# Attention scores on two row tiles of 64 array rows, their rows laid out in bands of 16 through device memory

## The chip, the cores and the metric

The kernel runs on one core of one Trainium2 chip. The metric is the device time of one execution in microseconds (us). TensorE (PE) multiplies matrices, VectorE (DVE) reduces and combines, ScalarE (ACT) evaluates exponentials and copies, GpSimd (POOL) does small elementwise work, and SyncE (SP) issues nearly all DMAs. Each engine works through its own instructions in order, and semaphores order the engines among each other.

## The reference

One transformer layer on x of shape (8, 256, 128). First comes attention with 16 heads of size 8, over 512 context positions and the element's own 256 positions; then a mixture of 8 experts, of which each token takes two. The change concerns the scores of the attention:

```python
q, k, v = (qkv[0], qkv[1], qkv[2])                 # (B, 16, 256, 8)
k = jnp.concatenate([extra_k, k], axis=2)          # 512 context keys + 256 own
attn = jnp.einsum('bhnd,bhmd->bhnm', q * scale, k)
attn = jax.nn.softmax(attn, axis=-1)
out = jnp.einsum('bhnm,bhmd->bhnd', attn, v)
out = out.transpose(0, 2, 1, 3).reshape(B, N, C)
x = x + out @ w_proj.T + b_proj
```

## The kernel before, in words

The attention runs over 32 **quads**: for each of the 8 batch elements (`b`), four groups (`r`, or `t`) of four heads. All engines follow the same outer loop, `steps`: in step `s` (with `b, r = divmod(s, 4)`) PE computes the exponentials' scores of quad `s` and the scores for the row maxima of quad `s+2`, so the maxima run two steps ahead.

**Rows of the matmul.** Keys and queries have 32 rows per quad (4 heads of 8). Each is split into a rounded part and a rest (`parts`), and the product of three combinations (high with high, high with rest, rest with high) gives back the precision. So the stationary and moving operands `keys` and `blocks` have 96 rows of products, and four more rows (`SUM_ROWS`) subtract the row maxima. `blocks` holds the queries masked per head (`masked`, made by `mask_queries`), so that one operand of 128 rows serves four heads at once. The rows are moved from `parts` and `masked` into `keys` and `blocks` by DMAs from SBUF to SBUF, in `spread_rows` and `spread_blocks` on SP: three DMAs of 96 KB, three of 128 KB and one of 8 KB per quad. They are issued at the end of a step, when all exponential matmuls of quad `s` are out (`exp_filled`), for quad `s+4`, whose maxima PE starts at the beginning of step `s+2`.

**A step on PE** has six groups `i`. Each holds two halves of one maximum unit (`max_half`, unit `w = i`) and two exponential units (`exp_unit`), in the order half, exp, half, exp. After group 1 stand the value products (`pv_tile`, 128 rows by 32 columns, four column tiles at a time) of the second half of quad `s-1`, after group 4 those of the first half of quad `s`. Before groups 3 and 4 stand small transposes (`transpose_maxima`, `transpose_out`).

**Who waits for whom.** ACT turns each of the 12 exponential units from a PSUM bank (`exp_ps`, two of them) into `probs`; DVE reduces each of the 6 maximum units from a pair of banks (`max_ps`, two pairs) into `max_part`. The merged maxima go from DVE to POOL (split in two), to PE (transposed), to ACT (`maxT`), and by a DMA of 8 KB on SP into `blocks`; the first exponential unit of the next step waits for it (`max_in`). POOL makes `parts` and `masked` for later batch elements (`split_context` in its steps r = 2, `split_own` in r = 3), in two buffers.

Of the kernel before, what the change touches and what calls it, by code (L numbers as in the profile page):

```python
# [85 lines left out]
OWN = NC_  # L86


def attend(nc, m, d):

# [11 lines left out]
    with ExitStack() as ctx:  # L102
# [13 lines left out]
        bias_added = sem("bias_added")  # L116
        rows_in, max_in = [sem(f"rows_in{t}") for t in range(T)], [sem(f"max_in{t}") for t in range(T)]
# [16 lines left out]
        parts = sb("parts", [P, 2, 2, NC_ + 2 * N], F32R)  # L134
        keys = sb("keys", [P, T, KEYS], F32R)
        masked = sb("masked", [P, 2, 2, G, N])
        head_hot, mask = sb("head_hot", [P, HEADS]), sb("mask", [P, G])
        blocks = sb("blocks", [P, T, G, N], F32R)
        ctx_v, own_v = sb("ctx_v_sb", [P, 2, CT, C]), sb("own_v", [P, 2, QT, C])
        value_cols = sb("value_cols", [P, T, KT, G, ROWS])  # L140
        max_part, rowmax = sb("max_part", [P, 2, 2, G, QT]), sb("rowmax", [P, 2, G, QT])
# [21 lines left out]
        def spread_blocks(engine, q):  # L163
            c, t = divmod(q, T)
            for j, part in enumerate((0, 0, 1)):
                engine.dma_start(blocks_f[ROWS * j:ROWS * (j + 1), t], masked[ROWS * t:ROWS * (t + 1), c % 2, part])\
                      .then_inc(rows_in[t], 16)

        def mask_queries(engine, c, part):
            spread = [P, G, N]  # L170
            return engine.tensor_tensor(masked[:, c % 2, part],
                                        parts_f[:, c % 2, part, KEYS:KEYS + N].unsqueeze(1).to_broadcast(spread),
                                        mask[:].unsqueeze(2).to_broadcast(spread), ALU.mult)

        rows_spread = lambda q: 16 * (6 + 7 * (q // T))

        @block.sync
        def _(sp):
# [3 lines left out]
            def spread_rows(q):  # L182
                c, t = divmod(q, T)
                high, rest = parts_f[:, c % 2, 0], parts_f[:, c % 2, 1]
                head = slice(ROWS * t, ROWS * (t + 1))
                for j, part in enumerate((high, rest, high)):
                    sp.dma_start(keys_f[ROWS * j:ROWS * (j + 1), t, :], part[head, 0:KEYS]).then_inc(rows_in[t], 16)
                if q:
                    spread_blocks(sp, q)
                if c:  # L190
                    sp.dma_start(blocks_f[SUM_ROWS:SUM_ROWS + 2, t], blocks_f[SUM_ROWS + 2:SUM_ROWS + 4, t])\
                      .then_inc(rows_in[t], 16)
# [927 lines left out]
```

## Time and profile before

| | |
|---|---|
| time, median of 3 runs | 581.93 us (579.75 to 582.76) |
| profiled execution, its own time | 579.1 us |
| its span in the trace | 577.5 us |
| PE busy | 498.9 us, 86% |
| DVE busy | 353.9 us, 61% |
| ACT busy | 292.7 us, 51% |
| POOL busy | 196.0 us, 34% |
| device memory read, written | 16.58 MB, 4.72 MB |

The attention takes the first 370 us or so of the span, the experts the rest. A busy PE is one with a matmul in its pipeline, which is not the same as one at its peak. The profiled execution lies 2.8 us under the median of the runs.

### The profile page before, as it was taken

The numbers are of one execution on the slowest core, as the hardware profiler recorded it, in microseconds if no ns is written. First come the engines' busy times: TensorE is split into PE (matmuls) and PEld (weight loads), VectorE is DVE, ScalarE is ACT, GpSimd is POOL, SyncE is SP. The second block draws the span as 40 slices with busy tenths as digits, with TensorE's granted clock in tenths as the row PEclk, the third lists the DMA queues.
The fourth block names the chain that finished last, engine by engine and source line by source line (L and its number), as shares of the span: only waits on it lengthen the run. The fifth ranks groups of instructions, "written<-read, shape, count | busy, mean of one in ns | idle before, by whom it ended". The sixth has DMA issues, their size and how long they took to land. (4 is left out here: it accounts for less than half of the span.)

```text
span 577.5 us, 10586 instructions
## 1 busy us (share of the span) xinstructions
PE 498.9 (86%) x3467; PEld 322.9 (56%) x3468; DVE 353.9 (61%) x646; ACT 292.7 (51%) x584; POOL 196.0 (34%) x381
## 2 busy tenths in 40 slices
PE   3479999999999999999999998555499999999940
PEld 1346666666666666666565663244447666666630
DVE  7597687777777787777777770368524333333316
ACT  2136667767767677676776767421023333333310
POOL 7151241331422412411400000103317776677630
PEclk9999999999999999999999999865569999999995
DMA  6802434445244344342332300160101111111116
GB/s 168 185 25 72 94 88 108 95 105 134 75 113 121 87 120 104 91 115 64 76 72 58 90 3 2 36 184 0 14 10 43 41 41 38 39 36 43 42 51 189
DMA packets 32078, 44.39 MB, mean 77 GB/s; under 512 B 5484, under 2 KB 20460, under 8 KB 32036
## 3 DMA queue, kind: packets, MB, share of 16 engines
q1 hardware_dynamic: 27076, 36.88, 25.7%
q0 software_dynamic: 2560, 5.25, 3.6%
q10 hardware_dynamic: 2400, 1.70, 1.2%
q8 instruction: 26, 0.43, 0.3%
q14 instruction: 16, 0.13, 0.1%
HBM read 16.58 MB, written 4.72 MB: 37 GB/s over the span
## 5 line engine op out<-in xcount | busy, mean ns | idle before, releaser
L426 DVE TENSOR_REDUCE max_part<-max_ps 128x2 f32<-128x1024 f32 (+1 forms) x192 | 231.3, 1221 | 79.6 <-PE max_ps L519 42.1
L385 ACT ACTIVATE probs<-exp_ps 128x512 f32<-128x512 f32 x384 | 207.4, 591 | 77.5 <-PE exp_ps L541 72.0
L541 PE MATMUL exp_ps<-blocks,keys 128*128 128x512 f32 x384 | 160.9, 421 | 4.5 <-ACT probs L385 2.3
L519 PE MATMUL max_ps<-keys,blocks 128*128 128x512 f32 x256 | 109.9, 436 | 10.1 <-DMA blocks<-masked 7.0
L541 PEld LDWEIGHTS exp_ps<-blocks,keys 128*128 128x128 f32 x384 | 71.7, 187 | 44.8 <-ACT probs L385 18.5
L551 PE MATMUL pv_ps<-probs,value_cols 128*32 128x256 f32 x1536 | 96.3, 383 | 0.0
L986 DVE TENSOR_TENSOR hidden<-up_ps,silu 128x512 f32<-128x512 f32 x40 | 27.7, 692 | 84.4 <-PE up_ps L1076 82.4
L302 POOL CAST maxes<-rowmax 128x8 fp32r<-128x8 f32 x32 | 6.3, 198 | 178.6 <-DVE rowmax L432 178.6
L519 PEld LDWEIGHTS max_ps<-keys,blocks 128*128 128x128 f32 x256 | 48.4, 191 | 30.2 <-DVE max_part L426 19.2
L551 PEld LDWEIGHTS pv_ps<-probs,value_cols 128*32 128x32 f32 x1536 | 43.3, 109 | 39.4 <-issue 17.1
L879 ACT ACTIVATE hiddenT<-at_ps 128x512 f32<-128x512 f32 x40 | 23.9, 597 | 77.2 <-PE at_ps L1093 68.7
L524 PE MATMUL max_ps<-keys,blocks 128*128 128x256 f32 x256 | 56.1, 303 | 1.6 <-DVE max_part L426 1.6
L524 PEld LDWEIGHTS max_ps<-keys,blocks 128*128 128x128 f32 x256 | 42.8, 189 | 10.2 <-DVE max_part L426 7.5
L1073 PE MATMUL gate_ps<-gate,xT 128*128 x80 | 44.4, 638 | 2.9 <-DVE xT L978 1.5
L1085 PEld LDWEIGHTS t_ps<-down,hiddenT 128*128 128x128 f32 x320 | 38.9, 192 | 14.0 <-issue 14.0
L823 POOL DMA_INDIRECT x_in<-h_rows,source_now x40 | 39.6, 989 | 17.1 <-issue 16.5
L1085 PE MATMUL t_ps<-down,hiddenT 128*128 x320 | 42.6, 276 | 2.1 <-ACT hiddenT L879 1.5
L847 POOL DMA_INDIRECT pick_outs<-y_out,target_now x40 | 39.6, 991 | 12.5 <-issue 10.2
L875 ACT ACTIVATE silu<-gate_ps 128x512 f32<-128x512 f32 x40 | 23.8, 596 | 37.5 <-PE gate_ps L1073 36.1
L1076 PE MATMUL up_ps<-up,xT 128*128 x80 | 42.6, 615 | 0.0
L264 POOL COPY value_cols<-ctx_v_sb 128x128 f32<-128x128 f32 x32 | 9.7, 304 | 68.8 <-PE pv_ps L551 66.8
L1076 PEld LDWEIGHTS up_ps<-up,xT 128*128 128x128 f32 x80 | 15.8, 197 | 20.2 <-issue 20.2
(148 smaller groups left out, 473.4 us busy)
## 6 DMA issues: line engine op xcount, KB each, us to landing
blocks<-masked SPq DMA_DIRECT2D x93, 128.0 KB
keys<-parts SPq DMA_DIRECT2D x96, 96.0 KB
ctx_v_sb<-ctx_v_dram SPq DMA_DIRECT2D x8, 256.0 KB, 2.9
gate<-gateT_dram SPq DMA_DIRECT2D x8, 256.0 KB, 2.8
up<-upT_dram SPq DMA_DIRECT2D x8, 256.0 KB, 2.6
y_in<-pick_outs SPq DMA_DIRECT2D x8, 256.0 KB, 4.9
raw<-ctx_kT_dram SPq DMA_DIRECT2D x7, 256.0 KB, 2.8
h_rows<-h SPq DMA_DIRECT2D x4, 256.0 KB, 4.9
```

Source lines behind the costliest of these rows:

```text
L385: act.activation(probs[par][:, k, 2 * half:2 * half + 2], exp_ps[u % 2][:].rearrange("p (g n) -> p g n", n=N), ACT.Exp).then_inc(exp_done, 1)
L426: vec.reduce_max(out, bank, axis=AX.X).then_inc(max_done, 1)
L519: mm = pe.matmul(max_ps[w % 2][:, half * BANK:(half + 1) * BANK], blocks[:, t, w, half * P:(half + 1) * P], keys[:, t, 0:NC_], start=True, ...
L524: mm = pe.matmul(max_ps[w % 2][:, first:first + N], blocks[:, t, 2 * (w - G) + half, i * P:(i + 1) * P], keys[:, t, NC_:KEYS], start=True, ...
L541: pe.matmul(exp_ps[u % 2][:], keys[:, t, k * P:(k + 1) * P], blocks[:, t, 2 * half:2 * half + 2, :], start=True, stop=True).then_inc(exp_f ...
L551: mm = pe.matmul(pv_ps[ROWS * g:ROWS * (g + 1), 0:N], value_cols[:, t, k, g, :], probs[q % 2][:, k, g, :], start=(k == 0), stop=(k == KT - 1))
L823: pool.indirect_dma_start(x_in[:, r, :], None, h_dram, bass.IndirectOffsetOnAxis(ap=source_now[:, r:r + 1], axis=0))\
L847: pool.indirect_dma_start(outs_dram, bass.IndirectOffsetOnAxis(ap=target_now[:, before2:before2 + 1], axis=0), y_out[:, before2, :], None) ...
L986: vec.tensor_tensor(hidden[:, r % 2, :], up_ps[r % 2][:], silu[:, r % 2, :], ALU.mult)\
L1073: pe.matmul(gate_ps[r % 2][:], xT[:, r % 2, :], m.gate[:, bass.ds(e, 1), :].rearrange("p a i -> p (a i)"), start=True, stop=True).then_inc ...
L1076: pe.matmul(up_ps[r % 2][:], xT[:, r % 2, :], m.up[:, bass.ds(e, 1), :].rearrange("p a i -> p (a i)"), start=True, stop=True).then_inc(up_ ...
L1085: mm = pe.matmul(y_ps[:, 0:C], hiddenT[:, r % 2, c, :], down[:, bass.ds(e, 1), c, :].rearrange("p a h -> p (a h)"), start=(c == 0), stop=( ...
```

## The change

The rows of a quad are laid out anew. A quad becomes two halves `a` of two heads each (`PAIR`), and each half has its own 64 rows (`TILE`): three bands of 16 rows (`BAND`) of products, 48 in all, and four more rows (two of which take the maxima). Half 0 uses rows 0 to 63, half 1 rows 64 to 127. The matmul instructions keep their number and their sizes in columns; each now contracts over 48 rows (maxima) or 64 rows (exponentials) instead of 128. On PE the order within a group becomes: maximum of half 1, exponential of half 0, maximum of half 0, exponential of half 1.

The rows come about in another way. Once per batch element SP writes `parts` and `masked` to device memory (`write_bands`: three DMAs of 384 KB and three of 256 KB, from 128 partitions each, with a destination of 8 blocks of 16 rows), waits for all six (`bands_in`), and reads the 48 rows of each half back (`read_bands`: four DMAs per quad, two of 96 KB and two of 144 KB). `parts` and `masked` now have one buffer, the device memory has two. The maxima go into `blocks` in two DMAs of 4 KB instead of one of 8 KB. `masked` has half as many columns, and at the start all of `masked` comes from 128x512 instead of 128x1024 operations; the DMAs that ACT issued at the start (`spread_blocks(act, 0)`) go.

```diff
+PAIR = G // 2
+TILE = P // 2
+BAND = PAIR * D
+MAX_ROW = 3 * BAND
...
+        key_bands = nc.dram_tensor("key_bands", (2, 2 * T, 3, BAND, KEYS), F32, kind="Internal").ap()
+        query_bands = nc.dram_tensor("query_bands", (2, 2 * T, 3, BAND, PAIR * N), F32, kind="Internal").ap()
...
+            def write_bands(c):
+                if c >= 2:
+                    for t in range(T):
+                        sp.wait_ge(rows_in[t], rows_spread(T * (c - 2)))
+                for j, part in enumerate((0, 1, 0)):
+                    sp.dma_start(key_bands[c % 2, :, j], parts_f[:, part, 0:KEYS]).then_inc(bands_in[c % 2], 16)
+                for j, part in enumerate((0, 0, 1)):
+                    sp.dma_start(query_bands[c % 2, :, j], masked[:, part]).then_inc(bands_in[c % 2], 16)
+
+            def read_bands(q):
                 c, t = divmod(q, T)
...
+                sp.wait_ge(bands_in[c % 2], bands_written(c))
+                for a in range(2):
+                    rows = slice(TILE * a, TILE * a + MAX_ROW)
+                    sp.dma_start(blocks_f[rows, t], query_bands[c % 2, 2 * t + a].rearrange("j i n -> (j i) n"))\
+                      .then_inc(rows_in[t], 16)
+                    sp.dma_start(keys_f[rows, t], key_bands[c % 2, 2 * t + a].rearrange("j i n -> (j i) n"))\
                       .then_inc(rows_in[t], 16)
...
-                    sp.dma_start(blocks_f[SUM_ROWS:SUM_ROWS + 2, q], maxT_f[:, (s + 1) % 2, :]).then_inc(max_in[q], 16)
+                    for a in range(2):
+                        row = TILE * a + MAX_ROW
+                        sp.dma_start(blocks_f[row:row + 2, q], maxT_f[2 * PAIR * a:2 * PAIR * (a + 1), (s + 1) % 2, :])\
+                          .then_inc(max_in[q], 16)
+                if r == 0 and b + 1 < B and b >= 0:
+                    sp.wait_ge(ctx_split, 2 * (b + 1) + 2)
+                    sp.wait_ge(own_split, 4 * (b + 1))
+                    write_bands(b + 1)
...
-                    c = (s + T) // T
-                    sp.wait_ge(ctx_split, 2 * c + 2)
-                    sp.wait_ge(own_split, 4 * c)
                     sp.wait_ge(exp_filled, (s + 1) * XUNITS)
-                    spread_rows(s + T)
+                    read_bands(s + T)
...
             def split_context(c):
                 pool.wait_ge(keysT_in[c % 2], 16 * (c // 2 + 1))
-                if c >= 2:
-                    for t in range(T):
-                        pool.wait_ge(rows_in[t], rows_spread(T * (c - 2)))
+                if c:
+                    pool.wait_ge(bands_in[(c - 1) % 2], bands_written(c - 1))
                 split(ctx_split, 2 * c, c, slice(0, NC_))
...
-                    mm = pe.matmul(max_ps[w % 2][:, half * BANK:(half + 1) * BANK], blocks[:, t, w, half * P:(half + 1) * P],
-                                   keys[:, t, 0:NC_], start=True, stop=True)
+                    g, i = divmod(w, QT)
+                    mm = pe.matmul(max_ps[w % 2][:, a * BANK:(a + 1) * BANK], blocks[rows, t, g, i * P:(i + 1) * P],
+                                   keys[rows, t, 0:NC_], start=True, stop=True)
...
-                pe.matmul(exp_ps[u % 2][:], keys[:, t, k * P:(k + 1) * P], blocks[:, t, 2 * half:2 * half + 2, :],
-                          start=True, stop=True).then_inc(exp_filled, 1)
+                pe.matmul(exp_ps[a][:], keys[rows, t, k * P:(k + 1) * P], blocks[rows, t], start=True, stop=True)\
+                  .then_inc(exp_filled, 1)
...
-                    for half in range(2):
+                    for a in range(2):
                         if has_scores(s + 2):
-                            max_half(s + 2, i, half)
+                            max_half(s + 2, i, 1 - a)
                         if has_scores(s):
-                            exp_unit(s, 2 * i + half)
+                            exp_unit(s, 2 * i + a)
```

The instructions of SP in the first step of a batch element and at the beginning of the next, before:

```order
L161 DMA raw<-ctx_kT_dram 128x512
L221 DMA blocks<-maxT 2x4x256
L224 DMA gate<-gateT_dram 128x512
L187 DMA keys<-parts 32x768 x3
L166 DMA blocks<-masked 32x1024 x3
L191 DMA blocks<-blocks 2x1024
L180 DMA ctx_v_sb<-ctx_v_dram 128x4x128
L221 DMA blocks<-maxT 2x4x256
```

The same place of SP in the changed kernel:

```order
L169 DMA raw<-ctx_kT_dram 128x512
L233 DMA blocks<-maxT 2x2x256 x2
L190 DMA key_bands<-parts 8x16x768 x3
L192 DMA query_bands<-masked 8x16x512 x3
L241 DMA gate<-gateT_dram 128x512
L199 DMA blocks<-query_bands 48x512
L201 DMA keys<-key_bands 48x768
L199 DMA blocks<-query_bands 48x512
L201 DMA keys<-key_bands 48x768
L183 DMA ctx_v_sb<-ctx_v_dram 128x4x128
L233 DMA blocks<-maxT 2x2x256 x2
```

The six writes stand between the step's maxima and the reads of the next element's first quad, and the next step's maxima (the last row) stand behind both.

SP at the start, before (the first rows of quads 0 and 1):

```order
L180 DMA ctx_v_sb<-ctx_v_dram 128x4x128
L187 DMA keys<-parts 32x768 x6
L166 DMA blocks<-masked 32x1024 x3
L187 DMA keys<-parts 32x768 x3
L166 DMA blocks<-masked 32x1024 x3
```

SP at the start in the changed kernel:

```order
L183 DMA ctx_v_sb<-ctx_v_dram 128x4x128
L190 DMA key_bands<-parts 8x16x768 x3
L192 DMA query_bands<-masked 8x16x512 x3
L199 DMA blocks<-query_bands 48x512
L201 DMA keys<-key_bands 48x768
L199 DMA blocks<-query_bands 48x512
L201 DMA keys<-key_bands 48x768
```

Where three direct copies of quad 0's keys went out first, the whole batch element is now written before the first row is read back.

## Rows read from the trace of the kernel before

**Rows 1.** The page: busy time of the engines; PE in 40 slices.

```profile
PE 498.9 (86%) x3467; PEld 322.9 (56%) x3468; DVE 353.9 (61%) x646; ACT 292.7 (51%) x584; POOL 196.0 (34%) x381
...
PE   3479999999999999999999998555499999999940
```

**Rows 2.** Timeline of PE in one step (start, duration, count).

```profile
240.71 0.40 PE L541 MATMUL exp_ps<-blocks,keys 128*128 128x512 f32 x1
241.04 1.50 PE L551 MATMUL pv_ps<-probs,value_cols 128*32 128x256 f32 x24
242.47 0.50 PE L524 MATMUL max_ps<-keys,blocks 128*128 128x256 f32 x2
242.81 0.39 PE L541 MATMUL exp_ps<-blocks,keys 128*128 128x512 f32 x1
```

**Rows 3.** Timeline of ACT, same step.

```profile
237.65 0.38 ACT L374 ACTIVATE pv_sb<-pv_ps 128x256 f32<-128x256 f32 x1 [0.86 <-PE pv_ps L551]
...
239.51 2.25 ACT L385 ACTIVATE probs<-exp_ps 128x512 f32<-128x512 f32 x4
243.24 1.09 ACT L385 ACTIVATE probs<-exp_ps 128x512 f32<-128x512 f32 x2 [1.49 <-PE exp_ps L541]
```

**Rows 4.** Timeline of DVE, same step.

```profile
241.20 1.22 DVE L426 TENSOR_REDUCE max_part<-max_ps 128x4 f32<-128x1024 f32 x1
243.48 1.23 DVE L426 TENSOR_REDUCE max_part<-max_ps 128x4 f32<-128x1024 f32 x1 [1.07 <-PE max_ps L524]
```

**Rows 5.** Timeline: first exponential matmul of steps 0 and 30; value products of last steps.

```profile
37.40 0.40 PE L541 MATMUL exp_ps<-blocks,keys 128*128 128x512 f32 x1
...
346.39 0.89 PE L541 MATMUL exp_ps<-blocks,keys 128*128 128x512 f32 x2 [0.30 <-ACT probs L385]
...
348.54 1.50 PE L551 MATMUL pv_ps<-probs,value_cols 128*32 128x256 f32 x24
...
358.13 1.50 PE L551 MATMUL pv_ps<-probs,value_cols 128*32 128x256 f32 x24
```

**Rows 6.** Timeline of weight loads, after a block of value products.

```profile
242.47 0.30 PEld L524 LDWEIGHTS max_ps<-keys,blocks 128*128 128x128 f32 x2 [0.41 <-DVE max_part L426]
```

**Rows 7.** Timeline: start of a batch element's first step on PE; DMA issues on SP.

```profile
243.51 0.40 PE L519 MATMUL max_ps<-keys,blocks 128*128 128x512 f32 x1
...
249.84 0.65 SPq L221 DMA_DIRECT2D blocks<-maxT  x1
253.98 1.81 SPq L187 DMA_DIRECT2D keys<-parts  x3
...
270.73 0.65 SPq L221 DMA_DIRECT2D blocks<-maxT  x1
```

**Rows 8.** Windows: engines, granted clock, busy share of 16 DMA engines, GB/s.

```profile
4.00:5.00 1.00, 0.00 (x0) 0.00 (x0) 0.32 (x2) 0.00 (x0) 1.00 (x2) 1.00 1.11 371
265.50:266.00 0.50, 0.50 (x5) 0.43 (x3) 0.50 (x1) 0.50 (x2) 0.41 (x2) 1.00 0.83 197
272.00:272.25 0.25, 0.25 (x5) 0.11 (x8) 0.21 (x3) 0.25 (x1) 0.00 (x0) 1.00 0.10 33
...
385.00:400.00 15.00, 4.16 (x18) 3.99 (x18) 12.02 (x33) 1.51 (x2) 0.87 (x2) 0.50 0.00 0
575.50:576.50 1.00, 0.00 (x0) 0.00 (x0) 0.00 (x0) 0.00 (x0) 0.00 (x0) 0.50 0.90 255
```

**Rows 9.** DMA issues: KB each, median us from issue to landing.

```profile
out_dram<-x ACTq DMA_DIRECT2D x4, 256.0 KB, 2.5
```

**Rows 10.** Timeline of the start, all engines.

```profile
13.25 2.44 DVE L171 TENSOR_TENSOR masked<-parts,mask 128x1024 f32<-128x1024 f32 x2
...
13.43 4.06 SPq L187 DMA_DIRECT2D keys<-parts  x6
...
21.55 1.19 PE L519 MATMUL max_ps<-keys,blocks 128*128 128x512 f32 x2 [7.03 <-DMA blocks<-masked]
...
26.61 0.72 PE L519 MATMUL max_ps<-keys,blocks 128*128 128x512 f32 x2 [0.82 <-DVE max_part L426]
```

More of the change, by code:

```diff
@@ L116, in attend @@
         bias_added = sem("bias_added")
+        bands_in = [sem(f"bands_in{i}") for i in range(2)]
         rows_in, max_in = [sem(f"rows_in{t}") for t in range(T)], [sem(f"max_in{t}") for t in range(T)]
@@ L255, in split_own @@
                     pool.wait_ge(own_split, 4 * c - 3 + part)
[L256 removed]
+                    mask_queries(pool, part).then_inc(own_split, 1)
             def fill_values(q):
@@ L277, in _ @@
                                pattern=[[-1, P]], channel_multiplier=1).then_inc(ident_done, 1)
-            for t in range(T):
-                pool.memset(blocks[:, t].bitcast(F32), 0.0).then_inc(blocks_zero, 1)
+            pool.memset(blocks[:].bitcast(F32), 0.0).then_inc(blocks_zero, 1)
             split_context(0)
@@ L510, in project_values, with max_half @@
                 mm.then_inc(v_filled, 1)
-            def max_half(q, w, half):
-                t = q % T
-                if w == 0 and half == 0:
+            def max_half(q, w, a):
+                t, rows = q % T, slice(TILE * a, TILE * a + MAX_ROW)
+                if w == 0 and a:
                     pe.wait_ge(rows_in[t], rows_spread(q))
-                if half == 0:
+                if a:
                     wait_for(pe, max_done, q * MUNITS + w - 1)
                 if w < G:
-                    mm = pe.matmul(max_ps[w % 2][:, half * BANK:(half + 1) * BANK], blocks[:, t, w, half * P:(half + 1) * P],
-                                   keys[:, t, 0:NC_], start=True, stop=True)
+                    g, i = divmod(w, QT)
+                    mm = pe.matmul(max_ps[w % 2][:, a * BANK:(a + 1) * BANK], blocks[rows, t, g, i * P:(i + 1) * P],
+                                   keys[rows, t, 0:NC_], start=True, stop=True)
                 else:
                     for i in range(QT):
-                        first = half * BANK + i * N
-                        mm = pe.matmul(max_ps[w % 2][:, first:first + N],
-                                       blocks[:, t, 2 * (w - G) + half, i * P:(i + 1) * P], keys[:, t, NC_:KEYS],
-                                       start=True, stop=True)
-                if half:
+                        first = a * BANK + i * N
+                        mm = pe.matmul(max_ps[w % 2][:, first:first + N], blocks[rows, t, w - G, i * P:(i + 1) * P],
+                                       keys[rows, t, NC_:KEYS], start=True, stop=True)
+                if a == 0:
                     mm.then_inc(max_filled, 1)
```

93 lines of the change are left out of this document (39 added, 54 removed).

## The prediction

> **What bounds the kernel now.** I read the page first: PE is busy 86% of the span and sits at 9 tenths in every slice of the attention [rows 1]. That invites the reading that PE sets the pace, so the second view is PE's timeline. From the first exponential matmul of step 0 at 37.40 to that of step 30 at 346.39 there are 308.99 us, 10.30 us a step. Steps 30 and 31 hold no maxima at all, half of PE's score work is gone, and yet the same place in two successive steps (the first value products) is 358.13 - 348.54 = 9.59 us apart [rows 5]. So PE's score matmuls are worth at most 10.30 - 9.59 = 0.71 us a step. What does set the pace is seen in ACT's timeline: four exponentials in 2.25 us, 0.56 us each, 6.7 us for twelve; and around each of the two blocks of value products ACT stands idle, 0.86 us before `pv_sb` and 1.49 us before the next exponential [rows 3]. The block takes 1.43 us of PE from its start at 241.04 to the next group at 242.47, and there are only two banks of scores in flight, so ACT runs out; the next exponential matmul starts another 0.34 us later, at 242.81 [rows 2]. DVE waits in the same place, 1.07 us [rows 4]. The pace is the loop of ACT, two banks and the value products, with DVE close by.
>
> **The matmuls.** Their number and columns stay; what can go is the time in which an exponential waits for the half before it. In the rows that is the 0.34 us after each block [rows 2], for ACT and for DVE, twice a step: at most 0.68 us, which is also what the steps without maxima say (0.71). Against it: `transpose_maxima` and `transpose_out` use the whole array and now stand between matmuls of half height. What a change of the array's division costs is seen after the value products (128x32): the next weight load comes 0.41 us after PE's previous one [rows 6], although the reduction it is put down to, of two units before, was long over. Four such changes a step are new, up to 1.6 us of PE; ACT's `maxT` and `pv_sb` copies cover most of it. I take a gain of 0.4 us a step (0.68 less a share of the four changes), 30 x 0.4 = 12 us in all, between 21 us (0.71) and nothing.
>
> The page "TensorEngine Tiling (Array Packing)" of the Trainium skill (Overview) gives up to 2x for a contraction of at most 64 rows. A pair of 512 columns each takes 0.43 us at 2.4 GHz, so by that alone the 12 pairs of a step would give back 2.6 us, and the sum would lose 77 us. The trace does not let it through, by the 9.59 us above. Its Key Properties say that changing the tiling mode drains TensorE; by that rule, the 0.41 us are a drain, and the trace agrees.
>
> **The writes, a new wait on SP.** Three DMAs of 384 KB and three of 256 KB are 1.97 MB. Nothing in the trace writes such rows to device memory, so the time T is bounded. Copies of the same 3 KB rows between SBUF tiles moved 197 GB/s at 0.83 of 16 engines' time, 14.8 GB/s an engine; loads 371 GB/s at 1.11, 20.9 GB/s an engine; the final stores lie between, 255 at 0.90, 17.7 [rows 8]. How many engines work at once? The DMA of `maxT`, two rows at its destination, moved its 8 KB in one quarter of a microsecond at a share of 0.10, 1.6 engines' worth [rows 8]: I read this as an engine for each of the two leading rows. A destination of 8 blocks then has 8 engines. T is 1.97 MB over 8 engines: 16.6 us at 14.8, 11.8 us at 20.9, 13.9 us at 17.7. I take 14. On all 16 engines T would be 8.3 to 5.3 us.
>
> The page "DMA: Bandwidth & Descriptors" of the Trainium skill (section on why a DMA increments its semaphore by 16) says that the engine count is the largest number up to 16 that divides both slowest dimensions; for 128 and 8 that is 8. No row shows a DMA with a leading 8.
>
> **Where SP stands meanwhile.** I count from the start of a batch element's first step on PE, 243.51, to the issue of the maxima, 249.84: 6.3 us [rows 7]. Two issues of 0.65 follow, to 7.6. From issue to data pass 1.4 us (issued at 270.73, moved from 272.00 to 272.25) [rows 7, 8], so data flow from 9.0 to 9.0 + 14 = 23.0; the landing of a store adds some 0.3 (2.5 us for 256 KB, of which 1.4 are the start and 0.9 the data) [rows 9], 23.3. Only then does SP pass `bands_in` and issue four reads at 0.60 to 0.62 each (three in 1.81 us) [rows 7], to 25.8, and one load, to 26.2. Behind them in SP's order stand the maxima of the *next* step. Their second DMA is issued at 26.85 and lands 1.5 later, at 28.35. PE wants them at the beginning of the second step after, at 2 x 9.9 = 19.8, plus 0.2 for the first maximum: 20.0. The first maxima of the new element want the read rows there too, and these arrive at 25.2 + 1.4 + 0.4 = 27.0. So PE, ACT and DVE stand 28.35 - 20.0 = 8.35 us, or T - 5.65. It happens once for each element that is still to be written, 7 times: 58 us. Nothing gives it back, since every step behind it has ACT's full length. Before, the rows went directly from SBUF to SBUF, and SP waited for no data between two sets of them.
>
> A stop of 8 us may also lower TensorE's clock. At the beginning, after a long idle, two 512-column matmuls took 1.19 us, later 0.72 [rows 10]; the thin stretch after the attention has the granted clock at 0.50, the 1.2 GHz level [rows 8]. If a stop does this, one block of value products (1.43 us) takes twice its time: 1.2 us each (between 0 and 2.4), 8 us.
>
> **The start.** The masked queries end at 13.25 + 2.44 = 15.69 [rows 10]; at half the columns at about 14.5. Data flow from 15.9 to 29.9, landed 30.2; the fourth read is issued at 32.1 and in at 33.9. The first maxima matmul was at 21.55 and waited for its rows then too [rows 10]: 12.3 us later, or T - 1.65. What follows it to step 0 is the same chain of reductions.
>
> POOL's new wait for `bands_in` in `split_context` falls into the same stop, a step or more before its product is used; nothing. The smaller `masked` operations are on POOL, 34% busy; nothing, their cover is its idle time.
>
> **The sum.** 579.1 (profiled execution, span 577.5 and 1.6 around it) - 12 + 58 + 8 + 12 = 645; the median of the runs shown lies 2.8 above the profiled one: 648. With T from 11.8 to 16.6, a step's gain from 21 to 0 and the clock from 0 to 17: 579.1 - 21 + 43 + 0 + 10 = 611, and 579.1 + 77 + 17 + 15 = 688.
>
> **The rivals.**
> - *All 16 engines write, and the gain stands* (not slower). T of 5.3 us: no stop, a start of +4: 579.1 - 12 + 4 = 571; at 8.3 us 7 x 2.65 + 7 - 12 gives 592. It turns where 7 (T - 5.65) + (T - 1.65) = 12, at T = 6.7 us, 296 GB/s. For it: loads did move 371 GB/s. Against it: only with 16 engines at full use, and the `maxT` row. 12 in 100 for faster or the same, 8 in 100 for 575 to 600.
> - *PE is the bound after all*: 12 pairs of 512 columns, 0.43 us each at the 2.4 GHz of the granted clock (1.00 in the windows of the attention [rows 8]), would take half: 2.6 us a step less, 77 us, which would turn 648 into 571. Against it stand steps 30 and 31. 2 in 100.
> - *The two halves do not overlap, or the changes of mode are all paid*: up to 1.6 us a step, 48 us, on top of the stops: 648 + 12 + 48 = 708, or some 640 where the writes are fast. For it the 0.41 us; against it ACT's copies. 10 in 100.
> - *A shorter stop*, because the six DMAs share engines better or SP is through sooner: 600 to 625. 13 in 100.
> - The forecast, 625 to 675: 55 in 100.
>
> **How the numbers follow.** About 0.5%, 3 us, is what a measurement of this kernel tells from none. Faster: 0.12, same: 0.03, slower: 0.85. The range from 592 to 690 leaves out most of the 16-engine rival below and the worst mode changes above.
>
> **What would show it.** Right: once per element, SP idle over 10 us for the DMAs of the bands, and right behind it one stop of PE of 6 to 11 us; the DMA share near 0.5 during the writes; the first maxima matmul near 34; between the stops steps of 9.6 to 10.2 us. A DMA share near 1 in the writes, or SP passing within 8 us, would make it wrong; so would steps under 9 us, or over 11.

## The result, and the profile after

The changed kernel takes 657.75 us (median of 4 runs, 651.18 to 660.53) where the kernel before, on the same chip, takes 582.35 (median of 4, 579.75 to 583.17). The ratio is 1.1287, with a 95% interval from 1.1187 to 1.1388: slower. The profiled execution took 660.21 us, with a span of 658.3; its mean granted clock is 0.868.

The page of the changed kernel, beside [rows 1]: busy time, the slices of PE, of its granted clock and of the DMA engines.

```profile
PE 519.4 (79%) x3467; PEld 299.9 (46%) x3468; DVE 353.7 (54%) x646; ACT 294.6 (45%) x584; POOL 180.4 (27%) x378
...
PE   2069899599699699699599699985565999999960
...
PEclk9999789788788989889979878976555999999995
DMA  5452413513622622532511421006001111111117
```

PE's slices are no longer even: from the eighth on, every third is a 5 or a 6. Its clock slices, too, are broken into 7s and 8s. DVE and ACT have the same busy time as before; what came in is standing still.

SP's timeline around one batch element's writes, issues alone:

```profile
259.71 1.27 SPq L233 DMA_DIRECT2D blocks<-maxT  x2
261.56 2.97 SPq L190 DMA_DIRECT2D key_bands<-parts  x3
264.57 5.43 SPq L192 DMA_DIRECT2D query_bands<-masked  x3
270.04 0.98 SPq L241 DMA_DIRECT2D up<-upT_dram  x1
275.44 0.33 SPq L199 DMA_DIRECT2D blocks<-query_bands  x1
275.81 0.42 SPq L201 DMA_DIRECT2D keys<-key_bands  x1
276.28 0.42 SPq L199 DMA_DIRECT2D blocks<-query_bands  x1
276.74 0.42 SPq L201 DMA_DIRECT2D keys<-key_bands  x1
...
277.68 1.38 SPq L233 DMA_DIRECT2D blocks<-maxT  x2
```

From the first write's issue to the first read's are 13.9 us. Only the last 4.4 of them (271.02 to 275.44) are idle waiting of SP for `bands_in`; the six writes and the load behind them took SP 9.4 us to issue. The maxima of the next step stand behind the reads and go out 18.0 us after their predecessors.

PE's timeline after that, and two other places: the start (beside [rows 10] and [rows 5]), and a block of value products in a step without a stop (beside [rows 2]).

```profile
34.75 0.79 PE L531 MATMUL max_ps<-keys,blocks 48*128 48x512 f32 x2 [18.70 <-DMA keys<-key_bands]
...
50.68 1.19 PE L553 MATMUL exp_ps<-blocks,keys 64*128 64x512 f32 x2
...
57.98 2.79 PE L563 MATMUL pv_ps<-probs,value_cols 128*32 128x256 f32 x24
...
280.06 0.79 PE L531 MATMUL max_ps<-keys,blocks 48*128 48x512 f32 x1 [6.45 <-DMA keys<-key_bands]
...
300.64 1.50 PE L563 MATMUL pv_ps<-probs,value_cols 128*32 128x256 f32 x24
302.07 0.39 PE L536 MATMUL max_ps<-keys,blocks 48*128 48x256 f32 x1
302.08 0.50 PE L553 MATMUL exp_ps<-blocks,keys 64*128 64x512 f32 x1
```

PE stands 6.45 us for `keys<-key_bands`. The block of value products at 57.98 took 2.79 us where it takes 1.50 at full clock: the attention begins at the lower level. At 302.07 and 302.08 a matmul for maxima and one for exponentials, on the two row tiles, start 0.01 us apart: the overlap is real, and the exponential no longer stands 0.34 us behind the maximum. The first exponential matmul is at 50.68, where it was at 37.40.

The windows of the changed kernel: the writes, the stop, and the two stretches behind it.

```profile
265.00:271.00 6.00, 6.00 (x51) 3.54 (x50) 5.27 (x7) 4.82 (x11) 1.56 (x5) 1.00 0.51 185
...
278.00:280.00 2.00, 0.00 (x0) 0.00 (x0) 0.00 (x0) 0.00 (x0) 0.00 (x0) 0.50 0.90 199
280.00:286.80 6.80, 6.74 (x36) 3.29 (x36) 2.45 (x2) 2.72 (x6) 0.00 (x0) 0.54 0.43 112
286.80:295.00 8.20, 7.89 (x66) 4.33 (x58) 5.59 (x8) 5.73 (x13) 2.50 (x5) 1.00 0.20 55
```

While the writes flow, the DMA engines are busy 0.51 of 16, that is 8 engines. In the stop, the clock falls to 0.50 (1.2 GHz), and for most of the 6.8 us of work behind it it stays there.

The chain of waits between 100 and 400 us of the changed kernel (in total, times, longest):

```profile
ACT probs L395 <- PE exp_ps L553: 99.1, 79, 7.6
DVE max_part L436 <- PE max_ps L531: 84.4, 43, 7.7
...
PE max_ps L531 <- DMA keys<-key_bands: 38.2, 6, 6.9
```

Six stops in this stretch, one for each element, and PE's releaser is the rows read back.

**Where the 80.8 us of span went.** Three places divide it: the first exponential matmul, the first statistics of the second layer norm (DVE, at 370.57 before and 448.66 after), and the end. The start is 13.3 us longer. The attention between the two places takes 397.98 us in place of 333.17: 64.8 more. The rest takes 2.7 more. In the attention DVE's idle times at the seven stops are 3.57, 7.71, 6.67, 6.80, 7.01, 7.17 and 6.46, 45.4 us. The distance between the first value products of successive steps, over an element's four steps at full clock, was 10.32, 10.74, 10.49 and 10.04; with row tiles it is 9.95, 10.38, 10.22 and 9.60: 0.36 us a step less, 10 us over 28 steps. (These four come from the version with both edits below; in the changed kernel itself the second always has a stop, and its other steps at full clock are 9.95, 10.21 to 10.24 and 9.58.) What is left, 64.8 - 45.4 + 10 = 29.4 us, I put to the clock; the experiments test that.

### The profile page after: what moved, and what is told of

It reads as the page before. It is cut to its first block and busy times, and to the rows that moved or that the text cites. A ratio compares the mean times of both kernels' runs of the same rounds, so it can differ in the third digit from the quotient of the medians.

```text
span 658.3 us, 10585 instructions
## 1 busy us (share of the span) xinstructions
PE 519.4 (79%) x3467; PEld 299.9 (46%) x3468; DVE 353.7 (54%) x646; ACT 294.6 (45%) x584; POOL 180.4 (27%) x378
## 5 line engine op out<-in xcount | busy, mean ns | idle before, releaser
L553 PE MATMUL exp_ps<-blocks,keys 64*128 64x512 f32 x384 | 171.3, 515 | 11.4 <-ACT probs L395 10.3
L531 PE MATMUL max_ps<-keys,blocks 48*128 48x512 f32 x256 | 114.3, 505 | 62.3 <-DMA keys<-key_bands 59.6
L563 PE MATMUL pv_ps<-probs,value_cols 128*32 128x256 f32 x1536 | 113.3, 435 | 0.0
L553 PEld LDWEIGHTS exp_ps<-blocks,keys 64*128 64x128 f32 x384 | 70.9, 201 | 47.1 <-issue 20.1
L531 PEld LDWEIGHTS max_ps<-keys,blocks 48*128 48x128 f32 x256 | 49.2, 218 | 93.4 <-DMA keys<-key_bands 42.4
L563 PEld LDWEIGHTS pv_ps<-probs,value_cols 128*32 128x32 f32 x1536 | 47.5, 121 | 48.9 <-issue 28.4
L536 PE MATMUL max_ps<-keys,blocks 48*128 48x256 f32 x256 | 48.5, 319 | 1.0 <-DVE max_part L436 1.0
L835 POOL DMA_INDIRECT x_in<-h_rows,source_now x40 | 39.4, 986 | 17.2 <-issue 16.6
L536 PEld LDWEIGHTS max_ps<-keys,blocks 48*128 48x128 f32 x256 | 32.2, 196 | 17.1 <-issue 9.3
L384 ACT ACTIVATE pv_sb<-pv_ps 128x256 f32<-128x256 f32 x32 | 12.3, 384 | 36.4 <-PE pv_ps L563 36.4
```

The source lines that it names most:

```text
L531: mm = pe.matmul(max_ps[w % 2][:, a * BANK:(a + 1) * BANK], blocks[rows, t, g, i * P:(i + 1) * P], keys[rows, t, 0:NC_], start=True, stop= ...
L536: mm = pe.matmul(max_ps[w % 2][:, first:first + N], blocks[rows, t, w - G, i * P:(i + 1) * P], keys[rows, t, NC_:KEYS], start=True, stop=True)
L553: pe.matmul(exp_ps[a][:], keys[rows, t, k * P:(k + 1) * P], blocks[rows, t], start=True, stop=True)\
L563: mm = pe.matmul(pv_ps[ROWS * g:ROWS * (g + 1), 0:N], value_cols[:, t, k, g, :], probs[q % 2][:, k, g, :], start=(k == 0), stop=(k == KT - 1))
L835: pool.indirect_dma_start(x_in[:, r, :], None, h_dram, bass.IndirectOffsetOnAxis(ap=source_now[:, r:r + 1], axis=0))\
```

## The experiments

The theory going in was the prediction's: the stop and the late start are the time of the writes on 8 engines, seen through SP's order; the row tiles themselves gain a little. Rivals: the loss is in the row tiles (changes of the array's division, no overlap) or in the clock.

**Sixteen engines for the writes.** The buffers in device memory get 128 leading rows, so that the writes' destinations do too; within a half the rows then lie head channel by head channel, which changes no sum:

```diff
-        key_bands = nc.dram_tensor("key_bands", (2, 2 * T, 3, BAND, KEYS), F32, kind="Internal").ap()
+        key_bands = nc.dram_tensor("key_bands", (2, P, 3, KEYS), F32, kind="Internal").ap()
...
-                    sp.dma_start(key_bands[c % 2, :, j], parts_f[:, part, 0:KEYS]).then_inc(bands_in[c % 2], 16)
+                    sp.dma_start(key_bands[c % 2, :, j, :], parts_f[:, part, 0:KEYS]).then_inc(bands_in[c % 2], 16)
```

> The writes get a destination whose leading dimension is 128 instead of 8; bytes, issues and their place stay. Theory (a DMA uses as many engines as its leading dimension allows, and SP's wait behind the writes makes the stop): the DMA share in the writes goes from 0.50 to near 1, SP's time from the first write's issue to the first read from 13.9 us to 8 to 9, the stop of DVE from 6.4 to 7.7 us to 0.5 to 2, the start 5 to 6 us earlier, and the time to 595 to 615 us. Rival (the rate into device memory or out of SBUF bounds the writes, not the number of engines): share near 1 but 13.9 us stays within 2 us, time above 640.

Measured: 596.49 us (594.69 to 598.47), ratio 1.0257 (1.0214 to 1.03). A window in its writes, and SP's issues:

```profile
220.00:224.00 4.00, 3.67 (x28) 2.29 (x32) 2.76 (x4) 2.84 (x6) 0.41 (x2) 1.00 1.02 394
```

```profile
218.90 1.35 SPq L190 DMA_DIRECT2D key_bands<-parts  x3
220.29 2.63 SPq L192 DMA_DIRECT2D query_bands<-masked  x3
...
227.03 0.32 SPq L199 DMA_DIRECT2D blocks<-query_bands  x1
```

The same bytes at the same place in SP's order now move at 394 GB/s (all traffic of the window) with a share of 1.02, and the first read is issued 8.1 us after the first write in place of 13.9. Up to the last steps, which have no maxima, no stop of DVE is longer than 2.7 us, and the first maxima matmul is at 27.4 in place of 34.75. So 61 of the 75 us hang on how many engines the writes get.

The page "DMA: Bandwidth & Descriptors" of the Trainium skill (section on why a DMA increments its semaphore by 16) has the engines as the largest number up to 16 that divides both slowest dimensions, 8 for 128 and 8, 16 for 128 and 128. The trace agrees, with 0.51 and 1.02.

**The writes earlier in SP's order.** Only their place changes, from behind the step's maxima to the beginning of the element's first step:

```diff
             def step(s, b, r):
+                if r == 0 and b + 1 < B and b >= 0:
+                    sp.wait_ge(ctx_split, 2 * (b + 1) + 2)
+                    sp.wait_ge(own_split, 4 * (b + 1))
+                    write_bands(b + 1)
```

> The six writes are issued at the beginning of the element's first step instead of behind the maxima of it, 7 us earlier; still 8 engines. Theory (SP's place makes the stop): the writes take the same 13.9 us, the stop falls below 1 us, the start stays as it is, time 590 to 615. Rival (the stop comes of the amount of data in the queues, wherever the writes stand): the stop stays at 5 us or more and the time within 15 us of the changed kernel's. If the clock falls only because of the stops, the granted clock rises from 0.87 to about 0.93.

Measured: 648.30 us (642.77 to 652.11), ratio 1.1178 (1.1107 to 1.1248). The theory of SP's order missed: the stop did not go, it moved, and the rival's figures came. The mean clock, 0.877 to 0.898 over the executions, did not rise to 0.93 either. SP's issues, ACT's copy of the maxima and PE's timeline, then PE's chain of waits between 100 and 360 us:

```profile
241.81 3.16 SPq L190 DMA_DIRECT2D key_bands<-parts  x3
245.02 5.33 SPq L192 DMA_DIRECT2D query_bands<-masked  x3
...
251.46 1.59 SPq L237 DMA_DIRECT2D blocks<-maxT  x2
```

```profile
245.69 0.36 ACT L389 ACTIVATE maxT<-shared_ps 8x256 fp32r<-8x256 f32 x1
```

```profile
256.08 0.80 PE L553 MATMUL exp_ps<-blocks,keys 64*128 64x512 f32 x2 [5.85 <-DMA blocks<-maxT]
```

```profile
PE exp_ps L553 <- DMA blocks<-maxT: 34.6, 6, 6.1
```

SP no longer waits for the end of the writes ahead of the maxima, but the issues themselves hold it. The maxima are ready at 246.05, when ACT's copy ends, and go out at 251.46, 5.4 us later; in steps without writes this takes 0.03 us. The six issues took 8.5 us, and the load behind them 1.0 where it takes 0.4 elsewhere. The 8 KB then land 4.6 us after the first of their two issues. In the version without a trip through memory (below), an exponential that waited for the same pair started 2.5 us after the first issue (326.35 to 328.84), so the transfer itself is some 2 us slower behind the writes. So six writes on 8 engines delay what stands behind them in two ways, and the larger is the time for which their issues hold the engine.

The page "DMA: Bandwidth & Descriptors" of the Trainium skill (section on queues, rings and completion order) says that each DMA engine consumes the descriptors of a ring in their order. The 2 us fit that, but no run here separates it from the mere sharing of the DMA engines.

**Both edits together.**

> Both edits. Theory: no stop, as with the early writes alone, so only the start gives more, 5 to 6 us: 584 to 609 us. Rival (fast writes still leave a part of a stop that the early ones don't): below the early one by more than 10 us.

Measured: 591.48 us (589.54 to 595.49), ratio 1.0198 (1.0144 to 1.0251). The expectation took for granted that the early writes alone leave no stop, and they did leave one; the 57 us between the two runs are its price and that of the start. No stop is left here, and the full steps are the 9.95, 10.38, 10.22 and 9.60 given above. Here the row tiles are seen without a stop: the start costs 43.28 - 37.40 = 5.9 us, and the attention takes 336.3 us where it took 333.2. The gain of 10 us a run is thus not just missing but overdrawn by 3; the 13 us against it go with a clock of 0.96 (windows below).

**The writes from POOL.** Built on the last: the writes of elements 1 to 7 are issued by GpSimd, behind its own `split_own`:

```diff
+                pool.wait_ge(ctx_split, 2 * c + 2)
+                pool.wait_ge(own_split, 4 * c)
+                write_bands(c)
```

> The kernel with writes on 16 engines, but those of elements 1 to 7 issued by GpSimd, right after it has made the rows, so they stand in neither SP's order nor its DMA queue. Theory (what the early writes left was the maxima's DMA standing behind the writes in one queue): no stop over 1 us, time 584 to 595, like that with both edits. Rival (the DMA engines themselves are shared, whatever the queue): maxima still late by 2 us or more, time above 600.

Measured: 594.70 us (591.75 to 594.96), ratio 1.0248 (1.0191 to 1.0305). No stop, the first maxima matmul at 27.29. The maxima are now issued within 0.03 us of ACT's copy in every step, where with both edits they are up to 2.4 us late behind the writes. Yet in four of the seven elements their packets begin to move only 1.9 to 2.4 us after the issue, where 1.25 is usual; with both edits it is 1.6 to 2.2. With 16 engines nothing more was to be had from another queue. Writes on 8 engines in another queue were not run.

**No trip through memory.** The bands go from SBUF to SBUF as before the change, but 16 rows at a time, 12 DMAs a quad, with `parts` and `masked` double:

```diff
+                    for j, (kp, qp) in enumerate(((0, 0), (1, 0), (0, 1))):
+                        rows = slice(TILE * a + BAND * j, TILE * a + BAND * (j + 1))
+                        sp.dma_start(keys_f[rows, t, :], parts_f[head, c % 2, kp, 0:KEYS]).then_inc(rows_in[t], 16)
+                        sp.dma_start(blocks_f[rows, t], masked[head, c % 2, qp]).then_inc(rows_in[t], 16)
```

> The two row tiles as in the change, but the bands go directly from SBUF to SBUF, twelve DMAs of 16 rows per quad, with two buffers for parts and masked as before; no device memory. Theory (row tiles give 0.7 us a step at full clock; the way over memory cost the start and the stops): first maxima matmul at 22 to 25 us, steps of 9.6 to 9.9, no stop, 21 us gained less some 10 for the clock: 565 to 580 us. Rival (twelve issues a step fill SP, 7.2 us of 9.6, and the last rows come late): PE waits for rows every step, time above 590.

Measured: 609.93 us (609.02 to 620.29), ratio 1.0508 (1.0432 to 1.0584). Two rows of its SP, and two of its chain of waits between 100 and 350 us:

```profile
261.60 0.59 SPq L192 DMA_DIRECT2D blocks<-masked  x1
262.23 0.59 SPq L191 DMA_DIRECT2D keys<-parts  x1
```

```profile
PEld exp_ps L542 <- DMA blocks<-maxT: 13.2, 12, 1.7
...
PE exp_ps L542 <- DMA blocks<-maxT: 6.9, 7, 1.4
```

The expected 565 to 580 us missed by 30, and the rival's figure (above 590) came. There is no 8 us stop, but twelve issues of 0.59 us back to back take 7.5 us of each step's 10, the maxima stand behind them, and steps last 9.95 to 13.7 us. The start shows it best: the first maxima matmul is early, at 24.79, and the first exponential is late, at 48.62. Writing whole bands to memory and reading 48 rows at 0.42 us an issue was the cheaper way for SP.

**No overlap of the halves.** Both halves of the score matmuls take the rows of tile 0, so that the products of tile 1's heads are left out:

```diff
-                t, rows = q % T, slice(TILE * a, TILE * a + MAX_ROW)
+                t, rows = q % T, slice(0, MAX_ROW)
...
-                rows = slice(TILE * a, TILE * (a + 1))
+                rows = slice(0, TILE)
```

> Both halves of a quad are computed from the rows of half 0, so that no two score matmuls lie on different rows of the array; the output is that of other scores, the work of every engine and every wait are the same. Theory (the overlap is worth about 0.7 us a step at full clock): steps of 10.2 to 10.6 us outside the stops instead of 9.6, time 675 to 690. Rival (the step is ACT's and DVE's alone, overlap is worth nothing): within 5 us of the changed kernel.

Measured: 739.6 us, from 713.08 to 763.57; its executions lie too far apart for a ratio, and only the kind of loss is read. Even 713.08 us is above the expected 675 to 690. The profiled execution is the one of 763.57 us, with a mean clock of 0.756; the one of 713.08 has 0.837, the changed kernel 0.868 to 0.888. A window of its attention, and its PE:

```profile
100.00:200.00 100.00, 99.84 (x515) 57.30 (x514) 50.30 (x62) 49.31 (x96) 16.41 (x38) 0.64 0.29 81
```

```profile
151.29 0.79 PE L531 MATMUL max_ps<-keys,blocks 48*128 48x512 f32 x1
151.88 0.62 PE L553 MATMUL exp_ps<-blocks,keys 64*128 64x512 f32 x1
152.31 0.62 PE L531 MATMUL max_ps<-keys,blocks 48*128 48x512 f32 x1
152.74 0.62 PE L553 MATMUL exp_ps<-blocks,keys 64*128 64x512 f32 x1
```

PE is busy 99.84 of 100 us, yet its clock is at 0.64 in the mean: 72 of these 100 us at the lower level, where 512 columns take 0.43 us. The size of 0.64 belongs to this execution; that the clock is lower than in the changed kernel holds for all four. I had expected the overlap's loss and the changes of mode alone. That the clock falls while PE is busy almost without a gap was in no theory.

The page "TensorE: Matmul & The Clock Gate" of the Trainium skill (Part 1) sets the clock by how busy TensorE has been. This measurement differs if busy means time in matmuls: 99.84% of the window held only 0.64.

**Half height alone.** The kernel before, with its score matmuls on rows 0 to 63 (the products of the other rows are left out), nothing else changed; so no overlap, no bands, the four changes of the array's division:

```diff
-                pe.matmul(exp_ps[u % 2][:], keys[:, t, k * P:(k + 1) * P], blocks[:, t, 2 * half:2 * half + 2, :],
+                pe.matmul(exp_ps[u % 2][:], keys[0:64, t, k * P:(k + 1) * P], blocks[0:64, t, 2 * half:2 * half + 2, :],
```

> The kernel before, with all score matmuls contracting over rows 0 to 63 only (the other 64 rows are left out, so the output is that of other scores); DMAs, waits, columns and counts stay. Theory (the clock falls because the half-height matmuls make the array work less, with or without a stop): no stop of DVE over 3 us, and yet stretches at 0.50 between steps, mean granted clock under 0.90, time 600 to 720 us. Rival (only the stops of the changed kernel lower the clock): clock 0.93 as before, and only the four changes of mode a step cost: 582 to 600 us.

Measured: 624.03 us (621.73 to 626.74), ratio 1.0766 (1.0699 to 1.0834). Weight loads of one step:

```profile
240.85 0.18 PEld L519 LDWEIGHTS max_ps<-keys,blocks 64*128 64x128 f32 x1 [0.41 <-DVE max_part L426]
...
241.96 0.23 PEld L533 LDWEIGHTS shared_ps<-ident_r,maxes 128*128 128x128 f32 x2 [0.36 <-issue]
...
243.39 0.20 PEld L559 LDWEIGHTS shared_ps<-ident,pv_sb 128*128 128x128 f32 x2 [0.36 <-issue]
243.75 0.29 PEld L524 LDWEIGHTS max_ps<-keys,blocks 64*128 64x128 f32 x2 [0.17 <-issue]
```

Before either full-array transpose there is a gap of 0.36 us that waits for nothing else; the same two loads in the kernel before (238.31 and 239.65) have none. The four steps of an element, at full clock, take 11.39, 11.81, 11.20 and 10.53 us, 44.93 together where 41.59 stood: 0.84 us a step, which I put to the changes of division when nothing overlaps. With overlap the steps are 0.36 shorter than before: against this kernel, the overlap, with the new order of the halves, is worth 1.2 us a step. The attention is 37.0 us longer; 30 steps at 0.84 are 25 of that, and 12 are left for a clock of 0.97 in the mean. I had expected a mean clock under 0.90 over the whole execution; it is 0.918 to 0.924, against 0.930 to 0.936 of the kernel before on the same chip. So the direction held in every execution and the size did not.

The page "TensorEngine Tiling (Array Packing)" of the Trainium skill (Key Properties) says that a change of mode drains TensorE. The trace agrees, with 0.36 us.

**The stops alone.** The other side of it: the kernel before at full height, with six 8-block writes per element and SP's wait for them before the row copies. They are read by nobody:

```diff
+            def write_bands(c):
+                for j, part in enumerate((0, 1, 0)):
+                    sp.dma_start(key_bands[c % 2, :, j], parts_f[:, c % 2, part, 0:KEYS]).then_inc(bands_in[c % 2], 16)
+                for j, part in enumerate((0, 0, 1)):
+                    sp.dma_start(query_bands[c % 2, :, j], masked[:, c % 2, part, 0:2]).then_inc(bands_in[c % 2], 16)
...
+                if c:
+                    sp.wait_ge(bands_in[c % 2], 96 * ((c + 1) // 2))
```

> The kernel before, at full height, with the change's six writes on 8 engines per element in SP's first step, and a wait for them ahead of the row copies of elements 1 to 7; what is written is not read. Theory (SP's wait makes the stop whatever the matmuls; half height makes the clock's loss after it larger): 7 stops of 6 to 9 us, 582 + 50 to 65 = 632 to 650 us, and the granted clock at 0.50 for less than 60 us of the attention, against 92 in the changed kernel. Rival (the clock's loss comes of the stops alone): as long at 0.50 as in the changed kernel, time 660 or more.

Measured: 648.39 us (645.48 to 650.41), ratio 1.1172 (1.1122 to 1.1223), with the start where it was (the first exponential matmul at 37.35). DVE's stops are 7.68, 7.73, 8.02, 7.89, 7.99, 7.55 and 6.79 us, 53.7 together. So the writes and one wait, without any row tile, make a kernel slower by 68 us.

The windows of the whole attention, from the first exponential matmul to the second layer norm, put the clock side by side: first the kernel before, then the changed kernel, both edits, half height alone, the stops alone.

```profile
37.40:370.57 333.17, 325.79 (x2634) 204.81 (x2632) 235.32 (x296) 232.30 (x480) 76.49 (x166) 1.00 0.34 82
```

```profile
50.68:448.66 397.98, 343.27 (x2634) 180.17 (x2634) 236.55 (x296) 232.98 (x480) 64.37 (x164) 0.88 0.31 89
```

```profile
43.28:379.57 336.29, 320.43 (x2634) 171.15 (x2634) 236.21 (x297) 232.87 (x480) 64.63 (x164) 0.96 0.35 105
```

```profile
42.42:412.56 370.14, 363.55 (x2634) 209.19 (x2632) 236.52 (x297) 236.60 (x480) 75.09 (x164) 0.97 0.30 74
```

```profile
37.35:435.70 398.35, 343.55 (x2634) 215.90 (x2632) 236.13 (x296) 233.57 (x480) 76.29 (x166) 0.92 0.38 103
```

A mean of 0.88 over 398 us is 95 us at the lower level; 0.96 over 336 is 27, and 0.92 over 398 is 64 (expected for the stops alone: under 60). For the half-height versions this is too little. Their profiles have no clock record before 61.0, 52.9 and 55.1, a window counts time without a record as full clock, and the value products there take twice their 1.50 us; so 10.3, 9.6 and 12.7 us at the lower level come on top. At full height the clock is up before the attention begins. PE's busy share does not explain half height alone: 363.55 of 370.14 us, 98.2%, at 0.97, against 325.79 of 333.17, 97.8%, at 1.00. Of the attention's extra time, the stops alone leave 65.2 - 53.7 = 11.5 us to the clock, and their other steps are exactly those of before, 10.32, 10.49 and 10.04 us. In the changed kernel it is 29, and steps without a stop are hit too: of one element's 9.95, 19.93, 11.48 and 11.15 us the last two are 1.3 and 1.6 us over their length at full clock. The stop, and the half height of the matmuls, each go with a lower clock, and together they do most.

**The maxima twice.** To see whether it is too little work on the array: the version with both edits, each 512-column maxima matmul issued twice, the second repeating the first.

```diff
-                    mm = pe.matmul(max_ps[w % 2][:, a * BANK:(a + 1) * BANK], blocks[rows, t, g, i * P:(i + 1) * P],
-                                   keys[rows, t, 0:NC_], start=True, stop=True)
+                    for _ in range(2):
+                        mm = pe.matmul(max_ps[w % 2][:, a * BANK:(a + 1) * BANK], blocks[rows, t, g, i * P:(i + 1) * P],
+                                       keys[rows, t, 0:NC_], start=True, stop=True)
```

> The kernel with early writes on 16 engines (591 us), with each of the 8 maxima matmuls of 512 columns in a step issued twice into the same bank. Theory (the clock falls because the half-height matmuls leave the array too little to do): the stretches at 0.50, 24 us of the attention there, fall under 8 us, while a step at full clock grows by 0.2 to 1 us; the time from 590 to 612 us. Rival (the clock falls for another reason, such as single waits): as many stretches at 0.50 as before.

Measured: 600.09 us (594.57 to 600.97), ratio 1.0298 (1.0241 to 1.0355). Its windows at the start, in the middle and in the last steps:

```profile
36.00:57.00 21.00, 19.09 (x94) 11.86 (x92) 15.96 (x18) 6.73 (x14) 6.40 (x12) 0.52 0.30 108
57.00:360.00 303.00, 299.57 (x2670) 178.96 (x2672) 231.25 (x280) 213.89 (x443) 63.94 (x158) 1.00 0.36 110
360.00:384.00 24.00, 21.96 (x130) 9.04 (x126) 0.86 (x4) 11.59 (x24) 0.00 (x0) 0.50 0.00 1
```

In the middle, where the doubled matmuls are, the clock is full without a break (0.97 without them in the same window). In the last steps, which have no maxima, it is at 0.50 for 24 us, where without them it is so for 10; at the start it is at 0.52, and the version without them has no clock record there to compare. The profiled execution took 600.97 us at a mean clock of 0.900; another, of 594.57 us, has 0.931, so the ends differ from one execution to the next. So the expected small total did not come, and the remedy holds only where it is applied. The doubling also fills gaps: PE is busy 299.57 of these 303 us, against 291.81 without it. So by itself this run shows that more matmul work brings the clock back, not that the height was what lacked. It costs more than it gives: the steps are 10.47, 10.89, 10.47 and 9.82 us.

**The start, and the transposes.** Two more on the version with both edits. In the first, quad 0's 32 rows are written and read ahead of the rest:

```diff
-            write_bands(0)
+            write_rows(0, slice(0, 2 * BAND), bands_first)
...
+            sp.wait_ge(bands_first, 96)
+            read_bands(0)
+            write_rows(0, slice(2 * BAND, P), bands_in[0])
```

> The kernel with early writes on 16 engines, and at the start quad 0's 32 rows written and read back ahead of the other 96. Theory (the start's delay is the writing of the whole element): first maxima matmul at 23.5 to 25 us instead of 27.3, time 587 to 589. Rival (twice as many issues eat it up): within 1 us of 591.5.

Measured: 589.50 us (587.07 to 590.2), ratio 1.015 (1.0112 to 1.0188), with the first maxima matmul at 24.78 and the first exponential at 40.72, 2.6 us earlier than without it. The start came as expected; the total is 2.0 us under that of both edits, which the intervals of the two ratios do not tell apart.

In the second, `transpose_out` also moves up beside `transpose_maxima`, with a place of its own in the bank, so that two of the four changes of division go:

```diff
+                        if s >= 1:
+                            transpose_out(s - 1)
                         transpose_maxima(s + 1)
```

> On top of the new start, both small transposes of a step stand together ahead of group 3, which leaves two changes of the array's division a step instead of four. Theory (the four changes cost 0.84 us a step): 0.2 to 0.4 us a step less, time 575 to 583. Rival (ACT's copies cover the changes once halves overlap): within 3 us of the one without; or the later normalization holds DVE up and it is slower.

Measured: 590.14 us (586.24 to 593.51), ratio 1.0152 (1.0103 to 1.0201), with steps of 9.95, 10.38, 10.23 and 9.58 us, unchanged. This is a miss: halving the number of changes gave nothing. That other work covers them once the halves overlap is the reading that is left, and it is argued, not measured. No version beat the kernel before; the best stays 1.5% behind.

## Why the prediction was right

The sign and the mechanism held: one stop per element (3.6 us the first, then 6.5 to 7.7), behind the bands in SP's order, a DMA share of 0.5 in the writes, and a late start. One sign did not come: SP was to be idle over 10 us for the bands, and it was idle 4.4, because issuing the writes and the load behind them held it for 9.4 us, which the prediction had nowhere. For the time from the first write to the first read this makes no difference; for the early writes it made most of it. Term by term:

- *The bound and the gain of a step.* Predicted 0.4 us, measured 0.36, 10 us in all. The reading of steps 30 and 31 was right, and PE was not the bound: the steps gained less than the 0.71 us that it allowed. What was wrong in the working is how it comes about: half height alone costs 0.84 us, and the overlap gives back 1.2, where I had 0.68 less a share of the changes.
- *The writes.* Eight engines, as read from the `maxT` row. That reading took the number of engines from one quarter of a microsecond with eight packets, and was in part luck. T came out smaller: first write to first read 13.9 us, where the prediction's terms (1.4, 14 and 0.3) give 15.7; 13.9 less the 1.7 us of start and landing is 12.2, inside 11.8 to 16.6.
- *The stops.* Predicted 7 of 8.35, measured 45.4 in sum, mostly 6.5 to 7.7. By the prediction's own rule, T - 5.65, a T of 12.2 gives 6.55. The rule held, and its input was 1.8 too high. The reads' issues, at 0.42 in place of 0.60, point the same way.
- *The clock.* Predicted 1.2 us a stop, 8 in all; the remainder is 29.4. This is the term that was mis-sized. I took one block of value products at twice its time. The windows show work at 1.2 GHz for most of 6.8 us behind a stop, and further stretches in steps without a stop, which the stops at full height do not have. That half the height of the matmuls would cost clock by itself stands in no term.
- *The start.* Predicted 12.3, measured 13.2 at the first maxima matmul. The masked queries ended later than I had them, and SP's first write went out at 16.16 where 14.5 was forecast; the shorter T gave part of that back.
- *The sum.* -10 + 45.4 + 29.4 + 13.3 and 2.7 behind the attention is 80.8 of span; predicted were -12 + 58 + 8 + 12 = 66. A stop term 13 too large and a clock term 21 too small partly cancelled; that the total came so near is luck to that extent. The median lies 10 us above the forecast and inside the range.

The rivals: with 16 engines I had 571 to 592 us, on the strength of a clock that stays up. (Its lower end takes the 371 GB/s as they stood, 5.3 us; 16 engines at 20.9 GB/s make 5.9, and the run gave 8.1 - 1.7 = 6.4.) The run with 16 engines took 596.49: no stop, but a start 5.9 us late, and an attention of 342.2 us at a clock of 0.96 that ate the gain. The two halves do overlap. That writes placed earlier in SP's order would remove the stop was my error after the fact: their issues hold SP wherever they stand, 5.4 us of the maxima's lateness, and some 2 us more pass in the transfer. The chances given add up to 92 in 100, and 0.15 for faster or the same is not the 12 of the one rival and 2 of the other.

What stays open: the 29.4 us are a remainder, not measured by themselves. That half-height matmuls lower the clock is shown by half height alone, at the same busy share of PE; the doubled maxima, which bring it back in the middle, also fill gaps. What exactly the chip counts is not shown. Nor is it shown whether the 2 us in the transfer of the maxima come of the shared queue or of the shared DMA engines. Nor is it settled why the part behind the attention takes 2.7 us more; in its first 29 us the clock is at 0.52 where it was 0.56.

## What to carry to other kernels

Before sending rows over memory, look at the leading dimension of the *destination* too: while the same 1.97 MB went out, the windows show 185 or 394 GB/s, and this was most of the loss here. When a bulk transfer is added to a queue that also carries small urgent ones, count three things: the waits of the engine that issues, the time for which the issues themselves hold it (8.4 us for six writes here), and the delay of the small transfer behind the bytes in flight. And before splitting the array, find out whether its matmuls set the pace, and price the clock: half-height matmuls can take back at 1.2 GHz what their overlap gives.

## What was not expected of the hardware

- TensorE's clock fell under half-height matmuls although the engine was busy all the time: 0.64 in the mean over 100 us with PE busy 99.84 us in the profiled execution without overlap, and 0.97 over the attention in half height alone, where the same kernel at full height has 1.00. Doubling the half-height maxima brought it to 1.00 in the steps that have them.
- With four more changes of the array's division and no overlap, a step takes 0.84 us more; with overlapping halves, leaving two of them out changed nothing.
- Maxima of 8 KB, ready while 1.97 MB went out on 8 engines from the same engine, were issued 5.4 us late and landed 4.6 us after that, against 0.03 and 2.5 without such writes.
- An issue took 0.42 us from memory to 48 rows and 0.59 from SBUF to 16 rows; writes with 8 leading blocks held SP 8.4 us for six, those with 128 leading rows 4.0.
